# Causal mask added by VectorE instead of a matmul, maximum subtracted by GpSimd, one exponential a sequence

## Chip, cores and metric

One core of a Trainium2 chip. The metric is the device time of one execution in microseconds (us), the median of three runs. The engines are TensorE (PE in the profile, PEld for its weight loads), VectorE (DVE), ScalarE (ACT), GpSimd (POOL) and SyncE (SP), which issues the DMAs. They run their own instruction queues in order and meet through semaphores.

## What is computed

One layer on 32 sequences of 64 tokens of width 1024: a projection with a LoRA chosen by the sequence's labeler, causal attention with rotary positions (32 heads, 8 key and value heads, head width 32), an output projection with a residual, and two mixtures of LoRA experts on top of two more projections. Of it the change touches the softmax of attention:

```python
scores = jnp.einsum('bhqd,bhkd->bhqk', q, k) / math.sqrt(HEAD_DIM)
causal = jnp.tril(jnp.ones((seq_len, seq_len), dtype=bool))
scores = jnp.where(causal[None, None, :, :], scores, jnp.float32(-1e+20))
attn = jax.nn.softmax(scores, axis=-1)
out = jnp.einsum('bhqk,bhkd->bhqd', attn, v)
```

## The kernel before

The 2048 tokens are 16 units of 128 tokens, two sequences each. Four stages follow each other. First, weights that are used one after the other are multiplied into one (a fold: L368 are its matmuls). Second, attention goes unit by unit. Third, a second fold for the feed-forward part. Fourth, that part, unit by unit. A product of two float32 numbers is made of three matmuls (high by high, high by low, low by high); ACT copies the high part of a tile, and DVE or POOL subtracts it from the whole to get the low part.

The change is in stage two, `attention`. Each engine runs `step(u, main, score, value, nxt)`. In step u, unit u is projected (`main`), unit v = u-1 gets its scores and softmax (`score`), and unit w = u-2 its values (`value`). Steps 2 to 14 are a loop; steps 0, 1, 15, 16 and 17 are written out. Steps 16 and 17 project nothing more; in their place they do the first part of the second fold (`fold2.first` on PE, `fold2.low_w` on DVE, `fold2.high_w` on ACT).

PE's order in a step is fixed: for each of 8 slices k of the contraction, three parts of `project`, and ahead of some of them other work, by the table `BESIDE`: transposes of the probabilities of w (L997) at k=0 and 1, attention times values (L1012) at k=1 and 2, transposes of the rotated queries and keys of v (L968) at k=2 and 3, `scores(v,0)` (L984) at k=4 part 0, `scores(v,1)` at k=5 part 1. `project` writes banks 0 to 3 of PSUM; at k=0 its part 0 is bank 0, part 1 bank 1, part 2 banks 2 and 3. Banks 0 and 1 wait for DVE to have moved the former unit's out (`bank_out`), banks 2 and 3 for `qkv_out`. At k=7, behind part 0, PE transposes the low-rank product (`transpose_down`, L1023), for which ACT must have copied it (`down`: L738), and behind the last part `up` (L1029) adds the low-rank product into the banks. Then DVE moves the banks out with the bias (L906, three instructions; the last one signals `qkv_out`).

Scores of a sequence b are two PSUM banks (128 x 1024 values; `s_ps`). Before each bank's twelve matmuls a matmul of two constant bf16 tiles, `mask_l` and `mask_r`, writes 0 or -1e20 (L979), and the scores are added onto it. DVE then reduces the maximum (L880) and subtracts it, from PSUM into `prob` (L882, semaphore `s_sub`). `scores(v,1)` uses the same two banks, so it waits for `s_sub` of sequence 0.

ACT's part: sequence 0 is taken in 16 exponentials of 128x64 that also sum (L677, each with an accumulator read), where the step is also `main`; sequence 1 in one exponential (L679), and DVE sums it (L822). DVE inverts the sums (L824), POOL multiplies (`normalise`, L768), and PE transposes at the start of the next step. Orders around it: ACT does `exp_scores(v,0)`, `exp_scores(v,1)`, then `low` for `down` (L738), `lows` (L741), and the high parts of the next unit's input. DVE does `less_max(0)`, `less_max(1)`, both `inverse_sum`, then `lows` (L898) and the three moves of L906. POOL does the two halves of the rotation (L775, L777), `split_x`, `normalise(v,0)`, `split_a`, `split_x`, `normalise(v,1)`. DVE's work at the start of a step is `probs_low` (`pt_l`, L806) and the rotation's products (L801).

Of the kernel before, what the change touches and what calls it, by code (L numbers as in the profile page):

```python
# [502 lines left out]
def attention(nc, a, sem, keep, psum, ring, c_h, c_l, a_raw, index, fold1, fold2):  # L503
# [3 lines left out]
    def sb(name, shape, dt=F32):  # L507
# [28 lines left out]
    mask_f = prob[:, 0, :, :, :].rearrange("p g c k -> p (g c k)")  # L536
# [6 lines left out]
    const_in, index_in, mask_ready = sem("const_in"), sem("index_in"), sem("mask_ready")  # L543
# [11 lines left out]
    s_done, s_max, s_sub, s_exp, s_sum, s_inv, s_norm = (  # L555
        sem(n) for n in ("s_done", "s_max", "s_sub", "s_exp", "s_sum", "s_inv", "s_norm"))
    pt_done, pt_high, pt_low = sem("pt_done"), sem("pt_high"), sem("pt_low")
    pv_done, pv_out, stored = sem("pv_done"), sem("pv_out"), sem("attn_stored")
    consts = [(b_bc[:, :], a["b_qkv"].partition_broadcast(P)), (cos[:, :], a["cos"]), (sin[:, :], a["sin"]),
              (hmask[:, :], a["hmask"]), (ident[:, :], a["ident"]), (mask_f[:, BANK:BANK + P], a["mask_l"]),  # L560
              (mask_f[:, 0:BANK], a["mask_r"])]

    def k_tiles():
        return keys[:, :].rearrange("p (n t) -> p n t", t=SEQ)
# [91 lines left out]
    def scalar(act):  # L656
# [11 lines left out]
            act.wait_ge(pt_done, 2 * w + b + 1)  # L668
            act.activation(pt_h[:, :, :, :, :].rearrange("p q j g t -> p q (j g t)"), t_ps[:, :, :], ACT.Copy).then_inc(pt_high, 1)

        def exp_scores(v, b, sums):

            act.wait_ge(s_sub, 2 * v + b + 1)
            if sums:
                for g in range(2):
                    for c in range(KVH):
                        last = act.activation(prob[:, 0, g, c, :], prob[:, 0, g, c, :], ACT.Exp, scale=SCALE, accum_out=ssum[:, 0, g, c:c + 1])  # L677
            else:
                last = act.activation(prob[:, b, :, :, :], prob[:, b, :, :, :], ACT.Exp, scale=SCALE)  # L679
            last.then_inc(s_exp, 1)  # L680

        def step(u, main, score, value, nxt):
            v, w = u - 1, u - 2
# [42 lines left out]
            if score:  # L726
                if not main:
                    fold2.high_w(act, 5)
                    fold2.high_w(act, 6)
                exp_scores(v, 0, main)  # L730
                if not main:
                    fold2.high_w(act, 7)
                exp_scores(v, 1, False)
            if main:
                act.wait_ge(low_done, u + 1)
                for b in range(BPU):
                    rows = slice(b * SEQ, (b + 1) * SEQ)
                    last = act.activation(low4[rows, :, :], down_ps[rows, b * LR:(b + 1) * LR].unsqueeze(1).to_broadcast([SEQ, 4, LR]), ACT.Copy, scale=LORA_SCALE)  # L738
                last.then_inc(low_copied, 1)
                act.wait_ge(low_t, u + 1)  # L740
                act.activation(lows[:, :], low_ps, ACT.Copy).then_inc(low_high, 1)  # L741
            if nxt:
                high_a(act, u + 1)
                high_x(act, u + 1, 1)
# [2 lines left out]
                fold2.high_w(act, 0)  # L747

        act.wait_ge(const_in, 16 * len(consts))
        act.activation(mask_r[:, :], mask_f[:, 0:BANK], ACT.Copy)  # L750
        act.activation(mask_l[:, :], mask_f[:, BANK:BANK + P], ACT.Copy).then_inc(mask_ready, 1)
        fold2.high_chunk(act, 0, 0)
        steps(act, step)

    def gpsimd(pool):
        def split_x(u, half):
            pool.wait_ge(x_high, 2 * u + half + 1)
            pool.tensor_tensor(x_l[:, ks(half), :], x_raw[:, ks(half), :], x_h[:, ks(half), :].bitcast(F32), ALU.subtract).then_inc(x_low, 1)  # L758
# [29 lines left out]
        split_x(0, 0)  # L788
        split_a(0)
        split_x(0, 1)  # L790
        pool.wait_ge(fold1.done, fold1.TILES * fold1.chunks)
        pool.memset(vb_h[:, :, :, :, :, :].bitcast(F32), 0.0).then_inc(vb_zero, 1)
        pool.memset(vb_l[:, :, :, :, :, :].bitcast(F32), 0.0).then_inc(vb_zero, 1)
        steps(pool, step)

    def vector(dve):
# [19 lines left out]
        def row(t, b):  # L816
            return t[:, b, :, :].rearrange("p g c -> p (g c)")

        def inverse_sum(v, b, summed=False):
            dve.wait_ge(s_exp, 2 * v + b + 1)  # L820
            if not summed:
                dve.tensor_reduce(row(ssum, b), flat(b), AX.X, ALU.add).then_inc(s_sum, 1)  # L822
                dve.wait_ge(s_sum, UNITS + b if isinstance(v, int) and v == UNITS - 1 else v + 1)
            dve.reciprocal(row(sinv, b), row(ssum, b)).then_inc(s_inv, 1)  # L824

        def step(u, main, score, value, nxt):
# [28 lines left out]
            if score:  # L855
# [19 lines left out]
                    fold2.low_w(dve, 4)  # L875
                scores = s_ps[:, :, :].rearrange("p g (c k) -> p (g c) k", k=SEQ)

                def less_max(b):
                    dve.wait_ge(s_done, 2 * v + b + 1)
                    dve.tensor_reduce(row(smax, b), scores, AX.X, ALU.max).then_inc(s_max, 1)  # L880
                    dve.wait_ge(s_max, 2 * v + b + 1)
                    dve.tensor_tensor(flat(b), scores, row(smax, b).unsqueeze(2).to_broadcast([P, 2 * KVH, SEQ]), ALU.subtract).then_inc(s_sub, 1)  # L882

                less_max(0)
                if main:
                    less_max(1)
                    inverse_sum(v, 0, True)
                else:
                    fold2.low_w(dve, 5)
                    inverse_sum(v, 0)  # L890
                    fold2.low_w(dve, 6)
                    less_max(1)
            if score and main:
                inverse_sum(v, 1)
            if main:
                dve.wait_ge(low_high, u + 1)
                rows = slice(2 * LR, 3 * LR)
# [5 lines left out]
                for n in range(NCH):  # L903
                    dve.wait_ge(qkv_done, NCH * u + n + 1)
                    to, bias = (t[:, n * BANK:(n + 1) * BANK].rearrange("p (o c) -> p o c", o=2) for t in (qkv, b_bc))
                    dve.tensor_tensor(to, out[n] if n < NCH - 1 else psum[:, 2:4, 0:FCH], bias, ALU.add).then_inc(bank_out if n < NCH - 1 else qkv_out, 1)  # L906

        fold2.low_chunk(dve, 0, 0)
        steps(dve, step)

    def tensor(pe):
# [59 lines left out]
        def scores(v, b):  # L971
            if b == 0:
                pe.wait_ge(qk_low, 3 * v + 3)
                pe.wait_ge(k_low, v + 1)
                need(pe, pv_out, 2 * v)
            else:
                pe.wait_ge(s_sub, 2 * v + 1)
            for g in range(2):
                pe.matmul(s_ps[:, g, :], mask_l[:, :], mask_r[:, :], start=True, stop=False)  # L979
                for q in range(QUADS):  # L980
                    o = s_ps[:, g, q * 4 * SEQ:(q + 1) * 4 * SEQ]
                    cols = slice(q * GRP + 2 * g, q * GRP + 2 * g + 2)
                    for n, (qq, kk) in enumerate(((q_h, k_h), (q_h, k_l), (q_l, k_h))):
                        mm = pe.matmul(o, qq[:, b, cols, :].rearrange("p g t -> p (g t)"), kk[:, q, b, :, :].rearrange("p c t -> p (c t)"),  # L984
                                       start=False, stop=q == QUADS - 1 and n == 2)
            mm.then_inc(s_done, 1)

        def transpose_p(v, b):
# [626 lines left out]
```

## Time and profile before

| | |
|---|---|
| Median of 3 runs | 1226.75 us (1225.2 to 1227.36) |
| Span of the profiled execution | 1224.6 us |
| PE busy | 1199.6 us |
| DVE busy | 602.9 us |
| ACT busy | 379.0 us |
| POOL busy | 303.9 us |
| Attention steps in the trace | about 160 to 603 us, two steps of the drain until 648 us |
| One turn of the loop | 28.34 us |

The page gives busy times by engine over the whole span, and the chain of work that ended last, followed back. A timeline row is: start in us, duration in us, engine, line of the kernel, operation, what it writes from what it reads, how many instructions; in square brackets the engine's idle time just before, and whose result ended it. Rows with a count above one are merged, and PE's durations contain a latency, so that the distance between the starts of two matmuls is what one costs. A share of busy time is an average over stages, so the rows of one turn are read for this change.

### The profile page before, as it was taken

The numbers are of one execution on the slowest core, as the hardware profiler recorded it, in microseconds if no ns is written. First come the engines' busy times: TensorE is split into PE (matmuls) and PEld (weight loads), VectorE is DVE, ScalarE is ACT, GpSimd is POOL, SyncE is SP. The second block draws the span as 40 slices with busy tenths as digits, with TensorE's granted clock in tenths as the row PEclk, the third lists the DMA queues.
The fourth block names the chain that finished last, engine by engine and source line by source line (L and its number), as shares of the span: only waits on it lengthen the run. The fifth ranks groups of instructions, "written<-read, shape, count | busy, mean of one in ns | idle before, by whom it ended". The sixth has DMA issues, their size and how long they took to land.

```text
span 1224.6 us, 20268 instructions
## 1 busy us (share of the span) xinstructions
PE 1199.6 (98%) x7424; PEld 1071.1 (87%) x7440; DVE 602.9 (49%) x1173; ACT 379.0 (31%) x1157; POOL 303.9 (25%) x182
## 2 busy tenths in 40 slices
PE   7999999999999999999999999999999999999997
PEld 7999988888888888888889998888888888888886
DVE  5222136767676766777773226344443333334443
ACT  4212124455545555555543224111111111111110
POOL 0000123433433344444220002222222222222220
PEclk9999999999999999999999999999999999999999
DMA  6111032111111111110312314111111111111100
GB/s 245 35 36 51 9 121 82 44 47 56 43 48 46 43 43 43 43 52 25 119 54 87 108 70 139 53 59 59 52 51 51 51 51 51 51 51 51 51 35 34
DMA packets 30003, 74.82 MB, mean 61 GB/s; under 512 B 4114, under 2 KB 8722, under 8 KB 29970
## 3 DMA queue, kind: packets, MB, share of 16 engines
q1 hardware_dynamic: 29970, 74.36, 17.6%
q8 instruction: 23, 0.38, 0.1%
q14 instruction: 10, 0.08, 0.0%
HBM read 57.57 MB, written 16.78 MB: 61 GB/s over the span
## 4 chain that ended last, share of the span: by engine, by line
PE 93%; DVE 3%; ACT 1%; DMA 1%; issue 1%; POOL 0%; SPq 0%; DVEq 0%; ACTq 0%
PE psum L949 21%; PE psum L368 21%; PE psum L1499 19%; PE psum L1454 14%; PE psum L984 4%; PE psum L1012 4%; PE psum L1471 2%; PE psum L997 2%; PE psum L1479 2%; PE psum L968 1%; PE psum L1487 1%; PE psum L979 1%; PE psum L1029 1%; ACT low L738 1%; DVE rot_t L801 1%
## 5 line engine op out<-in xcount | busy, mean ns | idle before, releaser
L368 PE MATMUL psum<-c_high_low,w_h 128*128 128x256 f32 (+1 forms) x1344 | 238.4, 288 | 9.6 <-ACT w_h L242 8.1
L368 PEld LDWEIGHTS psum<-c_high_low,w_h 128*128 128x128 f32 x1344 | 205.0, 193 | 10.0 <-DVE c_high_low L296 8.1
L1499 PE MATMUL psum<-fr_h,c_high_low 128*128 128x512 f32 (+1 forms) x768 | 212.6, 361 | 0.1
L949 PE MATMUL psum<-p_h,c_high_low 128*128 128x512 f32 (+1 forms) x768 | 196.4, 359 | 0.5 <-DVE qkv L906 0.5
L368 PE MATMUL psum<-c_high_low,w_l 128*128 128x256 f32 (+1 forms) x704 | 177.8, 279 | 2.1 <-DVE w_l L350 2.1
L1454 PE MATMUL psum<-w_h,c_high_low 128*128 128x512 f32 x512 | 170.2, 397 | 0.8 <-DVE w_l L1279 0.8
L1499 PEld LDWEIGHTS psum<-fr_h,c_high_low 128*128 128x128 f32 x768 | 136.5, 188 | 22.6 <-issue 0.3
L949 PEld LDWEIGHTS psum<-p_h,c_high_low 128*128 128x128 f32 x768 | 134.1, 189 | 13.4 <-issue 0.7
L1499 PE MATMUL psum<-fr_l,c_high_low 128*128 128x512 f32 (+1 forms) x384 | 138.3, 360 | 0.0
L368 PEld LDWEIGHTS psum<-c_high_low,w_l 128*128 128x128 f32 x704 | 127.6, 193 | 2.3 <-DVE w_l L350 2.3
L1337 POOL TENSOR_TENSOR x_out<-x,spare 128x1024 f32<-128x1024 f32 x16 | 38.8, 2423 | 350.3 <-DMA out<-x_out 331.4
L1454 PEld LDWEIGHTS psum<-w_h,c_high_low 128*128 128x128 f32 x512 | 96.1, 188 | 23.1 <-DVE w_l L1279 1.7
L949 PE MATMUL psum<-p_l,c_high_low 128*128 128x512 f32 (+1 forms) x384 | 105.0, 368 | 0.0
L758 POOL TENSOR_TENSOR c_high_low<-ring,c_high_low 128x512 fp32r<-128x512 f32 x32 | 41.8, 1307 | 240.7 <-ACT c_high_low L643 240.7
L1454 PE MATMUL psum<-w_l,c_high_low 128*128 128x512 f32 x256 | 99.9, 390 | 0.0
L768 POOL TENSOR_TENSOR prob<-prob,sinv 128x1024 f32<-128x1024 f32 x32 | 62.7, 1960 | 140.7 <-DVE sinv L824 140.7
L1499 PEld LDWEIGHTS psum<-fr_l,c_high_low 128*128 128x128 f32 x384 | 72.2, 188 | 10.4
L949 PE MATMUL psum<-end_h,c_high_low 128*128 128x320 f32 x256 | 76.4, 311 | 0.0
L677 ACT ACTIVATE prob<-prob 128x64 f32<-128x64 f32 x240 | 57.7, 242 | 55.6 <-DVE prob L882 55.6
L949 PEld LDWEIGHTS psum<-p_l,c_high_low 128*128 128x128 f32 x384 | 67.2, 192 | 6.3
L880 DVE TENSOR_REDUCE smax<-psum 128x16 f32<-128x1024 f32 x32 | 39.2, 1224 | 58.4 <-PE psum L984 58.4
L1400 DVE TENSOR_TENSOR lb_h<-psum,lb_h 128x128 fp32r<-128x128 f32 x32 | 9.3, 292 | 117.9 <-ACT lb_h L1301 117.9
(142 smaller groups left out, 1996.5 us busy)
## 6 DMA issues: line engine op xcount, KB each, us to landing
ring<-in_x_t SPq DMA_DIRECT2D x32, 256.0 KB, 2.7
attn_scratch<-ring SPq DMA_DIRECT2D x16, 512.0 KB, 2.6
ring<-attn_scratch SPq DMA_DIRECT2D x32, 256.0 KB, 2.8
ring<-in_x_tok SPq DMA_DIRECT2D x16, 512.0 KB, 3.3
out<-x_out SPq DMA_DIRECT2D x16, 512.0 KB, 3.2
ring<-in_wqkv_t SPq DMA_DIRECT2D x12, 512.0 KB, 4.5
ring<-in_last_t SPq DMA_DIRECT2D x10, 512.0 KB, 4.8
w_raw<-in_w_cond SPq DMA_DIRECT2D x8, 512.0 KB, 9.4
```

The source lines that it names most:

```text
L368: mm = pe.matmul(to, stationary, moving, start=start and n == 0, stop=k == KT - 1 and n == len(passes) - 1, skip_group_check=True)
L677: last = act.activation(prob[:, 0, g, c, :], prob[:, 0, g, c, :], ACT.Exp, scale=SCALE, accum_out=ssum[:, 0, g, c:c + 1])
L758: pool.tensor_tensor(x_l[:, ks(half), :], x_raw[:, ks(half), :], x_h[:, ks(half), :].bitcast(F32), ALU.subtract).then_inc(x_low, 1)
L768: pool.tensor_tensor(rows, rows, sinv[:, b, :, :].rearrange("p g c -> p (g c)").unsqueeze(2).to_broadcast([P, 2 * KVH, SEQ]), ALU.mult).th ...
L880: dve.tensor_reduce(row(smax, b), scores, AX.X, ALU.max).then_inc(s_max, 1)
L949: mm = pe.matmul(to, sx[:, k, :], moving(w, n, k), start=first, stop=False, skip_group_check=True)
L984: mm = pe.matmul(o, qq[:, b, cols, :].rearrange("p g t -> p (g t)"), kk[:, q, b, :, :].rearrange("p c t -> p (c t)"), start=False, stop=q ...
L997: mm = pe.transpose(t_ps[:, q, at:at + P], prob[:, b, g, c:c + 2, :].rearrange("p c k -> p (c k)"), ident[:, :])
L1012: mm = pe.matmul(s_ps[:, b, q * 4 * SEQ:(q + 1) * 4 * SEQ], vv[:, b, q, j, :, :].rearrange("p c d -> p (c d)"), pp[:, q, j, :, :].rearrang ...
L1337: pool.tensor_tensor(x1_out[:, :], x1[:, :], bb_bc[:, :], ALU.add).then_inc(x1_biased, 1)
L1454: mm = pe.matmul(w_ps[:, n, :], s[:, k, :], w[:, k, n * BANK:(n + 1) * BANK], start=k == 0 and s is at_h and w is wo_h, stop=k == KT - 1 a ...
L1499: mm = pe.matmul(b_ps[:, n, 0:cols.stop - cols.start], s[:, k, :], w[:, k, cols], start=first, stop=n == 2 and k == KT - 1 and s is x1t_l)
```

## The change

The matmuls of the mask and their constants are gone; the first score matmul of each quad's part now starts the accumulation itself. The mask, 64 x 64, is loaded twice into `hidden`, once for the partitions of each sequence. DVE adds it while it moves the scores from PSUM to `prob` (`s_masked`), and takes the maximum from `prob`. POOL subtracts the maximum in place (`s_sub`). ACT takes one exponential for each sequence and sums nothing; DVE sums both. `scores(v,1)` on PE waits for `s_masked` of sequence 0. DVE's `inverse_sum(v,1)` moves from ahead of `lows` to between the second and the third instruction of L906. ACT's `down` and `down_high` become functions; their place in its order stays. In step 16, DVE does the add and maximum of sequence 1 ahead of `inverse_sum(v,0)` instead of last.

```diff
-    mask_l = sb("mask_l", [P, P], BF16)
-    mask_r = sb("mask_r", [P, BANK], BF16)
+    hidden = sb("hidden", [P, SEQ])
...
+    consts += [(hidden[b * SEQ:(b + 1) * SEQ, :], a["mask_r"][0:SEQ, 0:SEQ]) for b in range(BPU)]
...
-        def exp_scores(v, b, sums):
+        def exp_scores(v, b):
 
             act.wait_ge(s_sub, 2 * v + b + 1)
-            if sums:
-                for g in range(2):
-                    for c in range(KVH):
-                        last = act.activation(prob[:, 0, g, c, :], prob[:, 0, g, c, :], ACT.Exp, scale=SCALE, accum_out=ssum[:, 0, g, c:c + 1])
-            else:
-                last = act.activation(prob[:, b, :, :, :], prob[:, b, :, :, :], ACT.Exp, scale=SCALE)
-            last.then_inc(s_exp, 1)
+            act.activation(prob[:, b, :, :, :], prob[:, b, :, :, :], ACT.Exp, scale=SCALE).then_inc(s_exp, 1)
...
+        def less_max(v, b):
+            pool.wait_ge(s_max, 2 * v + b + 1)
+            rows = prob[:, b, :, :, :].rearrange("p g c k -> p (g c) k")
+            pool.tensor_tensor(rows, rows, smax[:, b, :, :].rearrange("p g c -> p (g c)").unsqueeze(2).to_broadcast([P, 2 * KVH, SEQ]),
+                               ALU.subtract).then_inc(s_sub, 1)
...
             if score:
+                less_max(v, 0)
+                less_max(v, 1)
                 normalise(v, 0)
...
-                def less_max(b):
+                def masked(b):
                     dve.wait_ge(s_done, 2 * v + b + 1)
-                    dve.tensor_reduce(row(smax, b), scores, AX.X, ALU.max).then_inc(s_max, 1)
-                    dve.wait_ge(s_max, 2 * v + b + 1)
-                    dve.tensor_tensor(flat(b), scores, row(smax, b).unsqueeze(2).to_broadcast([P, 2 * KVH, SEQ]), ALU.subtract).then_inc(s_sub, 1)
-
-                less_max(0)
+                    dve.tensor_tensor(flat(b), scores, hidden[:, :].unsqueeze(1).to_broadcast([P, 2 * KVH, SEQ]),
+                                      ALU.add).then_inc(s_masked, 1)
+                    dve.wait_ge(s_masked, 2 * v + b + 1)
+                    dve.tensor_reduce(row(smax, b), flat(b), AX.X, ALU.max).then_inc(s_max, 1)
+
+                masked(0)
                 if main:
-                    less_max(1)
-                    inverse_sum(v, 0, True)
+                    masked(1)
+                    inverse_sum(v, 0)
                 else:
                     fold2.low_w(dve, 5)
+                    masked(1)
                     inverse_sum(v, 0)
                     fold2.low_w(dve, 6)
-                    less_max(1)
-            if score and main:
-                inverse_sum(v, 1)
...
                     dve.tensor_tensor(to, out[n] if n < NCH - 1 else psum[:, 2:4, 0:FCH], bias, ALU.add).then_inc(bank_out if n < NCH - 1 else qkv_out, 1)
+                    if score and n == NCH - 2:
+                        inverse_sum(v, 1)
...
             for g in range(2):
-                pe.matmul(s_ps[:, g, :], mask_l[:, :], mask_r[:, :], start=True, stop=False)
```

## Rows read from the trace of the kernel before

**Rows 1.** The page: DVE, ACT and POOL beside PE, and the chain by engine.
```profile
PE 1199.6 (98%) x7424; PEld 1071.1 (87%) x7440; DVE 602.9 (49%) x1173; ACT 379.0 (31%) x1157; POOL 303.9 (25%) x182
...
PE 93%; DVE 3%; ACT 1%; DMA 1%; issue 1%; POOL 0%; SPq 0%; DVEq 0%; ACTq 0%
```

**Rows 2.** Busy times of one turn: stretch, length, busy (instructions) by engine, clock, DMA.
```profile
461.12:489.46 28.34, 28.23 (x180) 25.24 (x180) 19.75 (x29) 15.28 (x56) 11.40 (x8) 1.00 0.13 46
```

**Rows 3.** Timeline of PE in that turn, inside `scores(v,0)`, around one mask matmul.
```profile
477.39 0.28 PE L984 MATMUL psum<-k_h,q_l 128*128 128x256 f32 x1
477.51 0.39 PE L979 MATMUL psum<-mask_r,mask_l 128*128 128x512 bf16 x1
...
477.86 0.28 PE L984 MATMUL psum<-k_l,q_h 128*128 128x256 f32 x1
```

**Rows 4.** Timelines of the same turn: softmax of sequence 1, up to `transpose_down`.
```profile
481.17 0.26 ACT L677 ACTIVATE prob<-prob 128x64 f32<-128x64 f32 x1 [3.66 <-DVE prob L882]
...
483.46 1.22 DVE L880 TENSOR_REDUCE smax<-psum 128x16 f32<-128x1024 f32 x1 [2.32 <-PE psum L984]
...
485.86 0.24 DVE L824 RECIPROCAL sinv<-ssum 128x16 f32<-128x16 f32 x1
...
485.97 1.06 ACT L679 ACTIVATE prob<-prob 128x1024 f32<-128x1024 f32 x1 [0.87 <-DVE prob L882]
...
486.18 1.91 POOL L768 TENSOR_TENSOR prob<-prob,sinv 128x1024 f32<-128x1024 f32 x1 [7.31 <-DVE sinv L824]
...
487.07 1.22 DVE L822 TENSOR_REDUCE ssum<-prob 128x16 f32<-128x1024 f32 x1 [0.96 <-ACT prob L679]
...
487.54 0.56 ACT L738 ACTIVATE low<-psum 64x128 f32<-64x128 f32 x2 [0.51 <-PE psum L949]
488.15 0.14 PEld L1023 LDWEIGHTS psum<-ident,low 128*128 128x128 f32 x1 [0.39 <-ACT low L738]
```

**Rows 5.** Timelines of the start of a step, one engine after the other.
```profile
461.56 1.89 DVE L906 TENSOR_TENSOR qkv<-psum,b_bc 128x512 f32<-128x512 f32 x3 [0.80 <-PE psum L1029]
463.98 1.23 DVE L806 TENSOR_TENSOR pt_l<-psum,pt_h 128x1024 fp32r<-128x1024 f32 x1 [0.53 <-ACT pt_h L669]
...
463.87 0.51 PE L949 MATMUL psum<-p_h,c_high_low 128*128 128x512 f32 x2
...
463.52 1.92 POOL L768 TENSOR_TENSOR prob<-prob,sinv 128x1024 f32<-128x1024 f32 x1
```

**Rows 6.** The page's groups: line, out<-in, count, busy, mean ns, idle before.
```profile
L1337 POOL TENSOR_TENSOR x_out<-x,spare 128x1024 f32<-128x1024 f32 x16 | 38.8, 2423 | 350.3 <-DMA out<-x_out 331.4
```

**Rows 7.** Timelines of step 16, one engine after the other.
```profile
602.86 0.88 PE L1029 MATMUL psum<-pb,lows 128*128 128x512 f32 x4
...
614.79 1.22 PE L368 MATMUL psum<-c_high_low,w_l 128*128 128x256 f32 x8 [2.11 <-DVE w_l L350]
...
634.20 1.09 PE L997 MATMUL psum<-ident,prob 128*128 128x128 f32 x8 [0.42 <-POOL prob L768]
...
605.20 1.21 DVE L350 TENSOR_TENSOR w_l<-wo_raw,w_h 128x1024 fp32r<-128x1024 f32 x1
606.33 1.22 DVE L806 TENSOR_TENSOR pt_l<-psum,pt_h 128x1024 fp32r<-128x1024 f32 x1
...
626.19 1.22 DVE L880 TENSOR_REDUCE smax<-psum 128x16 f32<-128x1024 f32 x1 [0.87 <-PE psum L984]
...
631.23 1.16 DVE L350 TENSOR_TENSOR w_l<-w_raw,w_h 128x1024 fp32r<-128x1024 f32 x1
...
631.39 2.76 POOL L768 TENSOR_TENSOR prob<-prob,sinv 128x1024 f32<-128x1024 f32 x1 [17.73 <-DVE sinv L824]
```

**Rows 8.** PE's wait in step 1 (timeline), and granted clocks behind two waits (busy times).
```profile
186.67 1.74 PE L968 MATMUL psum<-ident,roped 128*128 128x128 f32 x8 [1.97 <-POOL roped L777]
...
186.67:190.66 3.99, 3.99 (x17) 3.61 (x17) 2.01 (x5) 2.85 (x7) 0.00 (x0) 0.57 0.62 247
614.79:618.07 3.28, 3.28 (x28) 3.28 (x29) 3.28 (x3) 0.59 (x2) 0.00 (x0) 1.00 0.04 9
```

More of the change, by code:

```diff
@@ L533, in attention @@
     ident = sb("ident", [P, P])
-    mask_l = sb("mask_l", [P, P], BF16)
-    mask_r = sb("mask_r", [P, BANK], BF16)
-    mask_f = prob[:, 0, :, :, :].rearrange("p g c k -> p (g c k)")
+    hidden = sb("hidden", [P, SEQ])
     out = [psum[:, n, :].rearrange("p (o c) -> p o c", o=2) for n in range(2)] + [psum[:, 2, 0:FCH], psum[:, 3, 0:FCH]]
@@ L541, in attention @@
     low_ps = t_ps[:, 1, 0:P]
-    const_in, index_in, mask_ready = sem("const_in"), sem("index_in"), sem("mask_ready")
+    const_in, index_in = sem("const_in"), sem("index_in")
     x_in = [sem("x_in0"), sem("x_in1")]
@@ L554, in attention @@
     v_high, v_low, vb_zero, vb_high, vb_low = (sem(n) for n in ("v_high", "v_low", "vb_zero", "vb_high", "vb_low"))
-    s_done, s_max, s_sub, s_exp, s_sum, s_inv, s_norm = (
-        sem(n) for n in ("s_done", "s_max", "s_sub", "s_exp", "s_sum", "s_inv", "s_norm"))
+    s_done, s_masked, s_max, s_sub, s_exp, s_sum, s_inv, s_norm = (
+        sem(n) for n in ("s_done", "s_masked", "s_max", "s_sub", "s_exp", "s_sum", "s_inv", "s_norm"))
     pt_done, pt_high, pt_low = sem("pt_done"), sem("pt_high"), sem("pt_low")
@@ L559, in attention @@
     consts = [(b_bc[:, :], a["b_qkv"].partition_broadcast(P)), (cos[:, :], a["cos"]), (sin[:, :], a["sin"]),
-              (hmask[:, :], a["hmask"]), (ident[:, :], a["ident"]), (mask_f[:, BANK:BANK + P], a["mask_l"]),
-              (mask_f[:, 0:BANK], a["mask_r"])]
+              (hmask[:, :], a["hmask"]), (ident[:, :], a["ident"])]
+    consts += [(hidden[b * SEQ:(b + 1) * SEQ, :], a["mask_r"][0:SEQ, 0:SEQ]) for b in range(BPU)]
     def k_tiles():
@@ L669, in probs_high, with down, down_high @@
             act.activation(pt_h[:, :, :, :, :].rearrange("p q j g t -> p q (j g t)"), t_ps[:, :, :], ACT.Copy).then_inc(pt_high, 1)
-        def exp_scores(v, b, sums):
+        def exp_scores(v, b):
             act.wait_ge(s_sub, 2 * v + b + 1)
-            if sums:
-                for g in range(2):
-                    for c in range(KVH):
-                        last = act.activation(prob[:, 0, g, c, :], prob[:, 0, g, c, :], ACT.Exp, scale=SCALE, accum_out=ssum[:, 0, g, c:c + 1])
-            else:
-                last = act.activation(prob[:, b, :, :, :], prob[:, b, :, :, :], ACT.Exp, scale=SCALE)
-            last.then_inc(s_exp, 1)
+            act.activation(prob[:, b, :, :, :], prob[:, b, :, :, :], ACT.Exp, scale=SCALE).then_inc(s_exp, 1)
+        def down(u):
+            act.wait_ge(low_done, u + 1)
+            for b in range(BPU):
+                rows = slice(b * SEQ, (b + 1) * SEQ)
+                last = act.activation(low4[rows, :, :], down_ps[rows, b * LR:(b + 1) * LR].unsqueeze(1).to_broadcast([SEQ, 4, LR]), ACT.Copy, scale=LORA_SCALE)
+            last.then_inc(low_copied, 1)
+        def down_high(u):
+            act.wait_ge(low_t, u + 1)
+            act.activation(lows[:, :], low_ps, ACT.Copy).then_inc(low_high, 1)
         def step(u, main, score, value, nxt):
@@ L729, in step @@
                     fold2.high_w(act, 6)
-                exp_scores(v, 0, main)
+                exp_scores(v, 0)
                 if not main:
                     fold2.high_w(act, 7)
-                exp_scores(v, 1, False)
+                exp_scores(v, 1)
             if main:
[L735 to L741, printed above, removed]
+                down(u)
+                down_high(u)
             if nxt:
@@ L749, in scalar @@
         act.wait_ge(const_in, 16 * len(consts))
-        act.activation(mask_r[:, :], mask_f[:, 0:BANK], ACT.Copy)
-        act.activation(mask_l[:, :], mask_f[:, BANK:BANK + P], ACT.Copy).then_inc(mask_ready, 1)
         fold2.high_chunk(act, 0, 0)
@@ L817, in row, with inverse_sum @@
             return t[:, b, :, :].rearrange("p g c -> p (g c)")
-        def inverse_sum(v, b, summed=False):
+        def inverse_sum(v, b):
             dve.wait_ge(s_exp, 2 * v + b + 1)
-            if not summed:
-                dve.tensor_reduce(row(ssum, b), flat(b), AX.X, ALU.add).then_inc(s_sum, 1)
-                dve.wait_ge(s_sum, UNITS + b if isinstance(v, int) and v == UNITS - 1 else v + 1)
+            dve.tensor_reduce(row(ssum, b), flat(b), AX.X, ALU.add).then_inc(s_sum, 1)
+            dve.wait_ge(s_sum, 2 * v + b + 1)
             dve.reciprocal(row(sinv, b), row(ssum, b)).then_inc(s_inv, 1)
@@ L976, in scores @@
             else:
-                pe.wait_ge(s_sub, 2 * v + 1)
+                pe.wait_ge(s_masked, 2 * v + 1)
             for g in range(2):
-                pe.matmul(s_ps[:, g, :], mask_l[:, :], mask_r[:, :], start=True, stop=False)
                 for q in range(QUADS):
@@ L984, in scores @@
                         mm = pe.matmul(o, qq[:, b, cols, :].rearrange("p g t -> p (g t)"), kk[:, q, b, :, :].rearrange("p c t -> p (c t)"),
-                                       start=False, stop=q == QUADS - 1 and n == 2)
+                                       start=n == 0, stop=n == 2)
             mm.then_inc(s_done, 1)
@@ L1004, in attend @@
                 pe.wait_ge(vb_low, v + 1)
-                pe.wait_ge(s_sub, 2 * v + 2)
+                pe.wait_ge(s_masked, 2 * v + 2)
             n = 0
@@ L1019, in transpose_down @@
                 pe.wait_ge(const_in, 16 * len(consts))
-                pe.wait_ge(mask_ready, 1)
                 pe.wait_ge(fold1.out_low, fold1.chunks * fold1.TILES)
```

## The prediction

> **What bounds the kernel now.** I read the page's busy shares and its chain first: TensorE (PE) is busy 98% of the span and carries 93% of the chain that ended last [rows 1]. Then I took one turn of the attention loop: from the first `up` matmul at 461.12 us to the next at 489.46 us it lasts 28.34 us, of which PE is busy 28.23 us at a granted clock of 1.00, with DVE at 19.75, ACT at 15.28 and POOL at 11.40 us [rows 2]. So removing PE work pays in full, and any new wait of PE costs in full. But PE runs its queue in order and meets, once in each turn, places where a result of another engine comes just in time. The timelines of the other engines around those places decide this change. I call step u the turn in which unit u is projected and unit v = u-1 gets its scores. Scores and main work meet in steps 1 to 15; step 16 has scores and the first part of the next fold.
>
> **What goes from PE.** Sixty-four mask matmuls, four in each of 16 units, one ahead of each half of a sequence's scores. Their recorded 0.39 us is latency, not a price. Between the `k_h,q_l` matmul at 477.39 and the second matmul behind it with a mask between, at 477.86, lie 0.47 us; starts of neighbours lie 0.12 us apart (477.39 to 477.51), so two gaps without the mask are 0.24, and the mask cost 0.23 us [rows 3]. Bounds: not below 0.12 (a 256-column neighbour) and not above 0.39. Per step 4 x 0.23 = 0.92 us; steps 1 to 15: -13.8 us. Step 16 keeps the 0.46 us before its first scores, the rest disappears in a wait there. The two casts of the mask on ACT and the larger mask loads were at the stage's start, where PE did not wait for them: 0.
>
> **What the softmax chain becomes.** Before, for the second sequence: scores end at e = 483.42 (DVE starts at 483.46), reduce 1.22, subtract 1.23, exponential 485.97 to 487.03 [rows 4]. After: DVE adds the mask and moves the scores (PSUM and SBUF in, SBUF out). The nearest row is the `pt_l` subtraction of the same shape, 1.23 us [rows 5]. Then the maximum from SBUF: the nearest row is `ssum`, 1.22 us [rows 4]. POOL subtracts the broadcast maximum: the nearest row is `normalise`, the same shape and the same broadcast, 1.91 us [rows 4]; only the operation differs. I take it; bounds 2.42 (POOL's pass over two full inputs of that size) [rows 6] and 1.76 (what a `normalise` took from the moment DVE let it run, 632.39 to 634.15) [rows 7]. ACT's exponential stays 1.06. The first sequence's 16 exponentials with accumulator reads end, but they ran from 481.17 to 485.10 (ACT was idle 0.87 us ahead of 485.97), off the path, so they pay nothing; nor does the earlier start of `scores(1)`, which now waits for the first DVE pass alone, 1.27 us: PE has three parts of `project` to do before it and comes later anyway.
>
> **Wait 1: `transpose_down`.** ACT holds exp(v,1) ahead of `down`, so `down` cannot start before it. Before, exp(v,1) ended at 487.03, `down` then waited for PE until 487.54, and PE's `transpose_down` came at 488.15, its weight load waiting 0.39 us [rows 4]: e + 4.73. After: e + 0.04 + 1.23 + 0.03 (add) + 1.22 (maximum) + 0.08 (DVE to POOL, as 486.10 to 486.18) + 1.91 + 0.06 + 1.06 (exp), then 0.47 until both `down` activations are out and 0.05 to PE: e + 6.15. PE's own work between e and this point doesn't change. So the wait grows by 1.42 us, in steps 1 to 15: +21.3 us. What is queued behind it is the rest of the projection and `up`; `down_high` and `lows` follow in 1.3 us as before, with ACT and DVE free.
>
> **Wait 2: the third bank of the next unit.** DVE now does `inverse_sum(v,1)` between the second and the last `qkv` move. `up` starts at U = 461.12; DVE's three moves run from 461.56 to 463.45. PE comes to the pieces of banks 2 and 3, which need `qkv_out`, in the second matmul of the pair that starts at 463.87, some 464.10, U + 2.98 [rows 5]. That leaves 0.65 us of slack. Put in between are ssum 1.22 + reciprocal 0.25, together 1.47 us. PE waits 1.47 - 0.65 + 0.05 = 0.87 us, and the restart costs 0.1 (8 matmuls after a wait took 1.22 us [rows 7]; 7 spacings of 0.12 and one latency of 0.28 [rows 3] are 1.12): 1.0 us in the starts of steps 2 to 15, 14 x 1.0 = +14.0 us. Bounds: 0.6 if the move and the reduce overlap more than the rows show, 1.2 if not at all. Behind the inserted pair on DVE stand `pt_l`, the rotation and so POOL's `rotated`; all slip by 0.9, as PE does, so they are in time as before. `normalise(v,1)` now ends at about U + 5.2, PE's `transpose_p(v,1)` comes at U + 6.1: covered by 0.9. `normalise(v,0)` is done a microsecond before the next step, behind the two subtractions: 1.8 us of slack.
>
> **POOL and DVE together.** A DVE pass with both inputs in SBUF and a POOL pass stretch one another: POOL's `normalise` at 631.39 takes 2.76 us instead of 1.91 beside DVE's `w_l` pass at 631.23, which ends at 632.39 [rows 7]. A reduce with one input isn't stretched (487.07, 1.22 us, with POOL from 486.18 to 488.09), nor a pass that reads PSUM (463.98, 1.23 us, with POOL from 463.52) [rows 4, 5]. So in the loop the new POOL passes meet only passes that let them run; in step 16 they meet `low_w`.
>
> Two places of the Trainium skill bear on this. "SBUF — State Buffer", section "SBUF: two separate sides", says that VectorE with two SBUF inputs and GpSimd exclude one another for whole instructions; by that rule, too, the loop is free of it and step 16 isn't, and the trace agrees. "GPSIMD Engine Reference", section "Engine selection", says to put elementwise passes on VectorE, GpSimd being about twice as slow; the trace says 1.91 against 1.23, 1.55 times. With an estimate by the page, 2.46 us a pass, wait 1 would be 2.0 us and the total 8 us higher, some 1262.
>
> **Step 16.** Counted from the `up` matmuls ahead of it, U = 602.86. `qkv_out` is 1.47 late. DVE's `low_w(0)`, which stood right behind at 605.20, then meets `normalise(15,1)` on POOL (U + 3.3 to 5.2) and ends at U + 6.3. The DVE chain from there to `w_l` at 614.74, for which PE waited before (614.79), slips by what its `pt_l` slips, which ended at 607.55, U + 4.69, and now ends at U + 7.4: +2.7 us. Then -0.46 for masks. From the end of `scores(0)` (DVE's reduce starts 0.04 behind it, at 626.19) to `transpose_p(15,0)` at 634.20 were 8.05 us [rows 7]. After: maximum known at 2.5; `low_w(5)` holds POOL until 3.7; subtract until 5.5; exp until 6.6. `scores(1)` ends at 4.3, its add and maximum at 6.8, then POOL subtracts for sequence 1 until 8.8 ahead of `normalise(0)`, which ends at 10.7 or, behind `low_w(6)`, at 11.7. That is +2.7 to +3.6, say 3.2. Step 16: 2.7 - 0.46 + 3.2 = +5.4 us.
>
> **Sum.** -13.8 + 21.3 + 14.0 + 5.4 = +26.9 us. The profiled execution has a span of 1224.6 us; the median of the runs is 1226.75, 2.15 above, which I leave as it is. A turn becomes 28.34 - 0.92 + 1.42 + 1.0 = 29.84 us. 1224.6 + 26.9 + 2.15 = 1253.7.
>
> **Rivals.**
> Both waits covered, faster. PE is busy 28.23 of 28.34 us, so if the chain is hidden only the masks count: -14.2, 1212.5 us. This decides at one place: `transpose_down` stays in time if less_max takes under about 0.5 us on POOL, and `qkv_out` if the inserted pair takes under 0.65. Rows at 1.91 and 1.47 speak against. 4%.
> Only one wait is real (the other is filled because an engine starts earlier than I see): without wait 2, 1239.7; without wait 1, 1232.4. In order queues speak against. 13% together.
> The clock. After PE stood 1.97 us until 186.67 the granted clock over the next 3.99 us was 0.57, so most of it at 1.2 instead of 2.4 GHz, and 0.43 x 3.99 = 1.7 us were lost [rows 8]; after a wait of 2.11 us, until 614.79, it stayed at 1.00 [rows 7, 8]. Waits of 1.4 and 0.9 us come every turn now, 4.3 us apart. If a third of the 15 turns fall to the lower level: +8.5, 1262; all: 1279. 11%, together with POOL's subtraction at its upper bound (15 x 0.51 = +7.7, 1261).
> The change does something else than it says (the mask add or the sum read at another rate): 2%, on both sides.
> My forecast, both waits: 70%, own range 1247 to 1260.
>
> **Range and chances.** The forecast's range is 1247 to 1260. With the first of the two cases of a single wait (1239.7, from 1238) and the clock or a slow POOL in part of the turns, up to 1268, no more than 2 in 10 are left out: 1238 to 1268. About 0.2% is what a measurement of this kernel can tell from no change, and no case lies within it but a mix of misses: faster 0.05, same 0.03, slower 0.92.
>
> **What would show it.** In the profile after: no L979 rows; a turn near 29.8 us; PE idle of 1.4 to 1.8 us behind ACT's `low` in each step and of 0.9 us behind DVE's `qkv`; POOL near 15.2 us in a turn with two subtractions of 1.91 us; ACT's exponentials at 1.06 us. It would be wrong if `down` started before exp(v,1) was over, if POOL's subtraction cost far less or more than `normalise`, or if the clock row fell below 1.00.

## The result, and the profile after

The changed kernel takes 1252.08 us (median of 4 runs, 1249.72 to 1252.36) against 1226.05 us of the kernel before on the same chip: 1.0205 times as long, 95% interval 1.019 to 1.0219. The forecast was 1253.7 us.

The page of the changed kernel, busy times by engine and the chain that ended last by engine:

```profile
PE 1189.5 (95%) x7376; PEld 1062.4 (85%) x7376; DVE 621.7 (50%) x1188; ACT 334.8 (27%) x690; POOL 365.8 (29%) x214
...
PE 84%; DVE 9%; POOL 3%; ACT 2%; issue 1%; DMA 1%; DVEq 0%; ACTq 0%
```

The span grew from 1224.6 to 1247.9 us, while PE's busy time fell by 10.1 us: PE now stands. Its share of the chain fell from 93% [rows 1] to 84%, and DVE, POOL and ACT took the difference. The waits by releaser over the whole span (total us, times, longest) say where PE stands, in the loop twice a turn:

```profile
PE psum L1025 <- ACT low L678: 21.5, 16, 1.4
...
PEld psum L953 <- DVE qkv L908: 14.5, 14, 1.1
...
PE psum L953 <- DVE qkv L908: 9.0, 15, 0.7
```

One turn by engine (stretch, length, busy and instructions of PE, PEld, DVE, ACT and POOL, clock, DMA), from one `transpose_down` to the next, against [rows 2]:

```profile
470.00:499.62 29.62, 27.59 (x177) 24.63 (x177) 20.79 (x30) 12.40 (x25) 15.23 (x10) 1.00 0.13 44
```

It is 1.28 us longer, with PE busy 0.64 us less. POOL's 15.23 us are the 11.40 of before and two passes of 1.91. ACT is 2.9 us lighter, which brings nothing. The clock stayed at 1.00. Now the chain behind `scores(v,1)` in this turn (timelines), to be laid beside [rows 4]:

```profile
493.33 1.22 DVE L883 TENSOR_TENSOR prob<-psum,hidden 128x1024 f32<-128x1024 f32 x1 [1.87 <-PE psum L987]
494.59 1.22 DVE L886 TENSOR_REDUCE smax<-prob 128x16 f32<-128x1024 f32 x1
...
495.89 1.91 POOL L770 TENSOR_TENSOR prob<-prob,smax 128x1024 f32<-128x1024 f32 x1 [2.45 <-DVE smax L886]
...
497.83 1.06 ACT L672 ACTIVATE prob<-prob 128x1024 f32<-128x1024 f32 x1 [3.29 <-POOL prob L770]
498.80 0.54 ACT L678 ACTIVATE low<-psum 64x128 f32<-64x128 f32 x2
...
499.39 0.33 PE L1025 MATMUL psum<-ident,low 128*128 128x128 f32 x1 [1.43 <-ACT low L678]
```

From DVE's start to PE's transpose are 6.06 us; before, 483.46 to 488.15, they were 4.69 [rows 4]. ACT's `low` has no idle time in front of it: it was queued behind the exponential, and PE stood 1.43 us for it. And the start of the next step, against [rows 5]:

```profile
501.15 1.29 DVE L908 TENSOR_TENSOR qkv<-psum,b_bc 128x512 f32<-128x512 f32 x2 [0.80 <-PE psum L1031]
502.36 1.21 DVE L825 TENSOR_REDUCE ssum<-prob 128x16 f32<-128x1024 f32 x1
503.61 0.25 DVE L827 RECIPROCAL sinv<-ssum 128x16 f32<-128x16 f32 x1
503.78 0.63 DVE L908 TENSOR_TENSOR qkv<-psum,b_bc 128x512 f32<-128x512 f32 x1
...
504.46 0.39 PE L953 MATMUL psum<-p_h,c_high_low 128*128 128x256 f32 x1 [0.59 <-DVE qkv L908]
```

DVE's three moves are torn apart by the sum and the reciprocal, and PE stands before the third bank until the last move is done, 0.59 us.

### The profile page after: what moved, and what is told of

Read it like the earlier page. It is cut to its first block, busy times and chain, and to the rows that moved or that the text cites. A ratio compares the mean times of both kernels' runs of the same rounds, so it can differ in the third digit from the quotient of the medians.

```text
span 1247.9 us, 19736 instructions
## 1 busy us (share of the span) xinstructions
PE 1189.5 (95%) x7376; PEld 1062.4 (85%) x7376; DVE 621.7 (50%) x1188; ACT 334.8 (27%) x690; POOL 365.8 (29%) x214
## 4 chain that ended last, share of the span: by engine, by line
PE 84%; DVE 9%; POOL 3%; ACT 2%; issue 1%; DMA 1%; DVEq 0%; ACTq 0%
PE psum L368 21%; PE psum L1501 18%; PE psum L953 15%; PE psum L1456 14%; PE psum L1015 4%; PE psum L987 4%; POOL prob L770 2%; PE psum L1473 2%; DVE qkv L908 2%; PE psum L1481 2%; DVE prob L883 2%; DVE smax L886 2%; PE psum L972 1%; DVE ssum L825 1%; ACT prob L672 1%
## 5 line engine op out<-in xcount | busy, mean ns | idle before, releaser
L368 PE MATMUL psum<-c_high_low,w_h 128*128 128x256 f32 (+1 forms) x1344 | 241.2, 290 | 10.8 <-DVE c_high_low L296 8.1
L368 PEld LDWEIGHTS psum<-c_high_low,w_h 128*128 128x128 f32 x1344 | 207.8, 196 | 11.2 <-DVE c_high_low L296 8.0
L953 PE MATMUL psum<-p_h,c_high_low 128*128 128x512 f32 (+1 forms) x768 | 200.2, 361 | 9.0 <-DVE qkv L908 9.0
L754 POOL TENSOR_TENSOR c_high_low<-ring,c_high_low 128x512 fp32r<-128x512 f32 x32 | 41.8, 1307 | 237.1 <-ACT c_high_low L641 237.1
L770 POOL TENSOR_TENSOR prob<-prob,smax 128x1024 f32<-128x1024 f32 x32 | 61.9, 1934 | 88.6 <-DVE smax L886 88.6
L672 ACT ACTIVATE prob<-prob 128x1024 f32<-128x1024 f32 x32 | 33.9, 1059 | 134.5 <-POOL prob L770 134.5
L1329 POOL TENSOR_TENSOR c_high_low<-ring,c_high_low 128x512 fp32r<-128x512 f32 x32 | 41.2, 1308 | 97.4 <-ACT c_high_low L1272 97.4
```

The lines of the kernel that those rows point to most:

```text
L368: mm = pe.matmul(to, stationary, moving, start=start and n == 0, stop=k == KT - 1 and n == len(passes) - 1, skip_group_check=True)
L770: pool.tensor_tensor(rows, rows, smax[:, b, :, :].rearrange("p g c -> p (g c)").unsqueeze(2).to_broadcast([P, 2 * KVH, SEQ]), ALU.subtract ...
L953: mm = pe.matmul(to, sx[:, k, :], moving(w, n, k), start=first, stop=False, skip_group_check=True)
L1329: pool.tensor_tensor(at_l[:, ks(half), :], at_raw[:, ks(half), :], at_h[:, ks(half), :].bitcast(F32), ALU.subtract).then_inc(at_low, 1)
```

## The experiments

Theory: the change takes 0.9 us of matmuls from a turn, and two places where PE's queue meets another engine's queue give it back and more; the costs come from the order in the queues and from the length of the chain, not from the amount of work. Rivals: POOL and DVE have simply too much work; or PE is slowed (clock, contention); or the mask work was hidden anyway. All medians stand beside runs of the kernel before on the same chip, 1225.81 us for the first four variants of the table and 1226.27 us for the last four. "The change's 26" is 1252.08 less 1226.05 us.

Turns are measured from `transpose_down` in step 1 to the one in step 15, divided by 14. The drain is what follows, from there to the first matmul behind the attention stage:

| kernel | step 1, step 15 (us) | turn | drain | median |
|---|---|---|---|---|
| before | 204.66, 601.53 | 28.35 | 47.1 | 1226.05 |
| changed | 203.06, 617.87 | 29.63 | 54.2 | 1252.08 |
| down_first | 201.56, 597.29 | 28.27 | 57.3 | 1232.14 |
| sum_early | 205.37, 608.77 | 28.81 | 51.7 | 1237.94 |
| no_mask (from before) | 203.88, 588.26 | 27.46 | 46.7 | 1213.34 |
| half | 204.62, 595.27 | 27.90 | 47.1 | 1219.79 |
| masks_kept | 203.87, 631.28 | 30.53 | 55.0 | 1265.59 |
| both_orders | 203.53, 607.66 | 28.87 | 54.9 | 1240.25 |
| sum_moved (from before) | 205.09, 613.41 | 29.17 | 52.6 | 1242.77 |
| subtract_on_dve | 202.49, 607.21 | 28.91 | 55.6 | 1242.50 |

### Wait 1 alone away: ACT's order

```diff
                 if not main:
                     fold2.high_w(act, 7)
-                exp_scores(v, 1)
+                    exp_scores(v, 1)
             if main:
                 down(u)
                 down_high(u)
             if nxt:
                 high_a(act, u + 1)
+            if score and main:
+                exp_scores(v, 1)
+            if nxt:
                 high_x(act, u + 1, 1)
```

> The changed kernel with ACT's order turned round in steps 1 to 15: `down`, `down_high` and `high_a` ahead of the exponential of sequence 1. Theory (two in-order waits): PE's wait of 1.43 us at `transpose_down` goes in 15 steps, -21.4 us; POOL's `split_a` now stands behind a later `normalise(v,0)` and may cost 0.2 us a turn, +3: 1234 us (1230 to 1238), PE's wait behind ACT's `low` under 0.3 us each, wait 2 (0.6 us of PE idle behind DVE's `qkv`) unchanged. Rival (POOL's two subtractions are simply too much work, wherever they stand): the chain is as long as before, 1252 us. Rival (clock or contention slows PE's own matmuls): 1252 us.

Measured: 1232.14 us (1231.65 to 1232.78), ratio 1.0053 (1.0036 to 1.007). Every engine has the same work in it as in the changed kernel, and 19.7 of the 26 us are gone (6.3 left over the kernel before). The timelines of ACT and PE in a turn:

```profile
483.62 0.56 ACT L678 ACTIVATE low<-psum 64x128 f32<-64x128 f32 x2 [2.88 <-PE psum L956]
...
485.29 1.05 ACT L672 ACTIVATE prob<-prob 128x1024 f32<-128x1024 f32 x1
...
484.23 0.33 PE L1028 MATMUL psum<-ident,low 128*128 128x128 f32 x1
...
489.30 0.39 PE L956 MATMUL psum<-p_h,c_high_low 128*128 128x256 f32 x1 [0.41 <-DVE qkv L911]
```

ACT waits for PE again, not the other way round; PE's transpose has no idle time in front. The rivals of too much work and of a slow PE gave 1252 and fall. Wait 2 is a little shorter (0.41), since PE comes later by a wait of some 0.2 us for `split_a`. The turn, 28.27 us, is even shorter than before, so the 6.3 us that are left don't come from the loop. They come from the drain, 57.3 us against 47.1: PE stands there 2.10, 2.90 and 4.52 us, and from 613.29 to 615.00 and from 638.57 to 643.00, behind the last two, its granted clock was 0.50 (timeline):

```profile
602.46 2.17 PE L368 MATMUL psum<-c_high_low,w_h 128*128 128x256 f32 x16 [2.10 <-DVE qkv L911]
...
613.29 2.08 PE L368 MATMUL psum<-c_high_low,w_l 128*128 128x256 f32 x8 [2.90 <-DVE w_l L350]
...
638.57 1.75 PE L1003 MATMUL psum<-ident,prob 128*128 128x128 f32 x7 [4.52 <-POOL prob L767]
```

### Wait 2 alone away: DVE's order

```diff
+            if score and main:
+                inverse_sum(v, 1)
             if main:
                 dve.wait_ge(low_high, u + 1)
...
-                    if score and n == NCH - 2:
-                        inverse_sum(v, 1)
```

> The changed kernel with `inverse_sum(v,1)` back ahead of `lows` on DVE, as in the kernel before. Theory: wait 2 goes, 0.75 to 0.86 us in each of 14 turns and 1.5 to 2.8 us in step 16, -12 to -15 us; the sum now runs beside `down` and makes `lows` about 0.1 us later, +1 to +2: 1239 us (1236 to 1243). Wait 1 stays at 1.43 us. Rival (all the loss is wait 1 and the rest is noise of the drain): 1252 us. Rival (the sum pushes `lows` and so `up` late by its full 1.47 us): 1252 to 1260 us.

Measured: 1237.94 us (1237.83 to 1238.37), ratio 1.01 (1.0083 to 1.0116): 13.9 us less than the change's 26. PE's wait behind `low` is as it was, there is none behind `qkv` in the loop, and `up` comes 0.08 us later (1.41 instead of 1.33 behind the transpose). Timeline of PE:

```profile
493.52 0.33 PE L1025 MATMUL psum<-ident,low 128*128 128x128 f32 x1 [1.43 <-ACT low L678]
494.93 0.96 PE L1031 MATMUL psum<-pb,lows 128*128 128x512 f32 x4
```

Turns of 29.63 (changed), 28.27 (without wait 1) and 28.81 (without wait 2) give 1.36 us for wait 1 and 0.82 us for wait 2.

### Wait 2 alone in the kernel before

```diff
-            if score and main:
-                inverse_sum(v, 1)
...
                     dve.tensor_tensor(to, ...).then_inc(bank_out if n < NCH - 1 else qkv_out, 1)
+                    if score and n == NCH - 2:
+                        inverse_sum(v, 1)
```

> The kernel before, with only `inverse_sum(v,1)` moved between the second and the third `qkv` move on DVE. Theory: wait 2 alone, 0.75 to 0.86 us in 14 turns and 1.5 to 2.8 us in step 16: +12 to +15 us, 1239.5 us (1237 to 1242). Rival (wait 2 exists only since wait 1 shifts the engines): 1226 us.

Measured: 1242.77 us (1240.55 to 1245.08), ratio 1.0128 (1.0106 to 1.0149), +16.5 us, a little above the upper end of what was expected. The turn is as expected, 0.82 us longer. The rest is in the drain, 5.5 us longer where 1.5 to 2.8 were expected: PE's 2.90 us wait for `w_l` there is followed by a stretch at the lower of its two clock levels (timeline and busy times):

```profile
629.42 2.07 PE L368 MATMUL psum<-c_high_low,w_l 128*128 128x256 f32 x8 [2.90 <-DVE w_l L350]
...
629.42:631.00 1.58, 1.58 (x7) 1.58 (x8) 1.58 (x2) 0.00 (x0) 0.00 (x0) 0.50 0.00 0
631.00:633.00 2.00, 2.00 (x11) 2.00 (x10) 1.77 (x2) 0.00 (x0) 0.00 (x0) 0.50 0.11 39
633.00:635.00 2.00, 2.00 (x11) 2.00 (x11) 0.00 (x0) 0.65 (x2) 0.00 (x0) 0.50 1.00 274
```

The profiled execution took 1244.71 us; two of the four took 1240.55 and 1240.83 us, inside what was expected, with a mean clock over the program of 0.997 and 0.999 instead of 0.995. So moving one sum of 1.47 us from a place with slack to right ahead of a move that PE waits for costs more than 1% of the kernel, without a microsecond of added work.

### The price of the mask on PE, from both kernels

From the kernel before, the masks left out (the causal mask is then missing from the scores):

```diff
-                pe.matmul(s_ps[:, g, :], mask_l[:, :], mask_r[:, :], start=True, stop=False)
...
-                                       start=False, stop=q == QUADS - 1 and n == 2)
+                                       start=n == 0, stop=n == 2)
```

> The kernel before, with the 64 mask matmuls left out and nothing else changed: the causal mask is missing from the scores. It prices what the change takes from PE. Theory (a mask matmul costs PE 0.22 us, and PE's work is paid in full): 15 x 0.89 + 0.45 = -13.8 us, 1212 us (1210 to 1215). Rival (0.39 us each, by the recorded duration): 1202 us. Rival (it hides under waits or weight loads): above 1220 us.

Measured: 1213.34 us (1212.53 to 1214.05), ratio 0.99 (0.9884 to 0.9917), -12.5 us. The turn falls from 28.35 to 27.46 us, 0.22 us for each of its four mask matmuls.

And into the changed kernel, the masks put back beside DVE's add (the reverse of that diff, with the constants of before):

> The changed kernel with the 64 mask matmuls put back on PE as well, so that the mask is added twice (the value is as good as minus infinity either way). Theory: wait 1 is counted from the end of `scores(v,1)`, so mask matmuls ahead of it lengthen the turn in full and the saving of the change is real but outweighed: +13.8 us, 1266 us (1263 to 1268). Rival (the waits have become the bound and the mask work would hide in them): 1252 to 1256 us.

Measured: 1265.59 us (1264.11 to 1267.21), ratio 1.0323 (1.0306 to 1.034), 13.3 us over the change's 26. The turn is 0.90 us longer, and PE's wait behind `low` stays at 1.42:

```profile
509.21 0.33 PE L1033 MATMUL psum<-ident,low 128*128 128x128 f32 x1 [1.42 <-ACT low L682]
```

A wait that is counted from the end of PE's own work doesn't hide that work. The saving is real in both kernels, and the rival of the hidden mask falls. The turn also adds up: 28.35 - 0.89 for the masks + 1.36 + 0.82 for the waits is 29.64 us, against 29.63 measured.

### POOL's part in wait 1

```diff
                 less_max(v, 0)
-                less_max(v, 1)
+                if not main:
+                    less_max(v, 1)
...
                 if main:
                     masked(1)
+                    dve.wait_ge(s_max, 2 * v + 2)
+                    dve.tensor_tensor(flat(1), flat(1), row(smax, 1).unsqueeze(2).to_broadcast([P, 2 * KVH, SEQ]), ALU.subtract).then_inc(s_sub1, 1)
                     inverse_sum(v, 0)
```

> The changed kernel with the subtraction of sequence 1 on DVE instead of POOL in steps 1 to 15. Theory: the chain behind `scores(v,1)` loses 0.08 + 1.91 + 0.06 and gets 0.03 + 1.22 + 0.03 us, 0.77 shorter, so wait 1 shrinks from 1.43 to 0.66 us: -11.6 us, 1240.5 us (1238 to 1243). Rival (wait 1 is all of POOL's making, and goes with it): 1231 us. Rival (POOL has nothing to do with it): 1252 us.

Measured: 1242.50 us (1238.58 to 1244.29), ratio 1.0129 (1.0103 to 1.0155), 9.8 us less than the change's 26; the turn is 0.72 us shorter. The wait halves and doesn't go:

```profile
491.61 0.33 PE L1030 MATMUL psum<-ident,low 128*128 128x128 f32 x1 [0.70 <-ACT low L680]
```

So of wait 1 one half is GpSimd in the place of VectorE (1.91 against 1.23 us for the subtraction, and the hand over to POOL). The other half is left of the pass that was added, three passes behind each other where there were two: 1.22 us, of which the 0.51 us that `low` waited for PE before [rows 4] cover a part.

### Both orders changed

The diff of ACT's order and, on DVE, `n == NCH - 1` in the place of `n == NCH - 2`.

> The changed kernel with both orders changed: on ACT `down`, `down_high`, `high_a` ahead of the exponential of sequence 1, on DVE `inverse_sum(v,1)` behind the last `qkv` move instead of ahead of it. Theory: both waits go, but the sum is then 1.5 us late for `normalise(v,1)` and delays `pt_l`; PE would wait about 0.6 us at `transpose_p(v,1)` and 0.2 us for `split_a` in each turn: turn 28.3 us, 1229 us (1224 to 1235). Rival (the costs add wherever the work stands): 1245 us or more.

Measured: 1240.25 us (1238.75 to 1240.61), ratio 1.0109 (1.0092 to 1.0126). This one I missed: 1229 was expected, up to 1235. The waits at `low` and at `qkv` are gone, and the one that was expected at the transposes of sequence 1 is not there. But the trace has new ones, in front of both groups of matmuls that read `pt_l`, 0.17 and 0.80 us (timelines of DVE, POOL, PE):

```profile
495.79 1.21 DVE L828 TENSOR_REDUCE ssum<-prob 128x16 f32<-128x1024 f32 x1
...
497.53 1.23 DVE L813 TENSOR_TENSOR pt_l<-psum,pt_h 128x1024 fp32r<-128x1024 f32 x1 [0.24 <-issue]
498.67 1.28 DVE L808 TENSOR_TENSOR roped<-qkv,cos 128x640 f32<-128x640 f32 x1
...
503.82 1.21 DVE L813 TENSOR_TENSOR pt_l<-psum,pt_h 128x1024 fp32r<-128x1024 f32 x1
...
497.37 1.90 POOL L767 TENSOR_TENSOR prob<-prob,sinv 128x1024 f32<-128x1024 f32 x1 [1.01 <-DVE sinv L830]
...
505.09 0.75 PE L1018 MATMUL psum<-pt_l,vb_h 128*128 128x256 f32 x4 [0.80 <-DVE pt_l L813]
```

I had followed the late sum through POOL, where `normalise(v,1)` is in time, and had named the delay of `pt_l` but given it no price: on DVE's own queue `pt_l(0)`, four rotation passes and `pt_l(1)` stand behind the sum. In the changed kernel they had slipped too, but PE had slipped with them, by wait 2. Now PE isn't late and waits for them instead, and the first rotation pass, which reads two SBUF tensors, runs longer into `normalise` on POOL (1.28 us; 1.04 in the changed kernel). So this order doesn't give back both waits: the length of the chain comes out at a third place. Whether another order would is not shown.

### Half of the change

Sequence 0 has 4.8 us of lead on sequence 1 (DVE starts on their scores at 502.06 and 506.85 us in the turn below). So it can take the longer chain, while sequence 1 keeps the short one.

```diff
+            with_mask = b == 1 or last_unit
...
             for g in range(2):
+                if with_mask:
+                    pe.matmul(s_ps[:, g, :], mask_l[:, :], mask_r[:, :], start=True, stop=False)
...
                 if main:
-                    masked(1)
+                    masked(0)
+                    less_max(1)
                     inverse_sum(v, 0)
+                    inverse_sum(v, 1)
```

`masked(0)` adds the mask and takes the maximum, and POOL subtracts; `less_max(1)` is maximum and subtraction on DVE, as in the kernel before.

> Sequence 0 of steps 1 to 15 by the new way (mask added by DVE, maximum subtracted by POOL, one exponential, sum by DVE), sequence 1 and all of step 16 by the old way, with its mask matmuls; `inverse_sum(v,1)` ahead of `lows`. Theory: sequence 0 has 4.8 us of lead on sequence 1, so its longer chain meets no wait of PE; half of the mask work is saved: 15 x 0.445 = -6.7 us, 1219.5 us (1217 to 1223), PE without a wait behind ACT's `low` over 0.4 us. Rival (POOL's subtraction or the added DVE sum costs wherever it stands): above 1230 us.

Measured: 1219.79 us (1218.4 to 1221.21), ratio 0.9948 (0.9931 to 0.9965): faster than both kernels, by 0.5% against the one before. One turn, and the places that matter in it (busy times; timelines):

```profile
484.96:512.87 27.91, 27.80 (x178) 25.00 (x178) 20.83 (x30) 12.40 (x25) 13.32 (x9) 1.00 0.14 47
...
510.67 1.16 DVE L836 TENSOR_REDUCE ssum<-prob 128x16 f32<-128x1024 f32 x1
511.86 0.25 DVE L838 RECIPROCAL sinv<-ssum 128x16 f32<-128x16 f32 x1
512.22 0.29 DVE L919 TENSOR_TENSOR lows<-psum,lows 32x128 fp32r<-32x128 f32 x1
...
511.55 0.33 PE L1047 MATMUL psum<-ident,low 128*128 128x128 f32 x1
```

DVE has as much work as in the changed kernel (20.83 against 20.79 us), and PE is busy 27.80 of 27.91 us. Both sums end in front of `lows`, with 0.11 us to spare. The turn is 0.45 us below that of before: two mask matmuls. The drain is that of before.

## Why the prediction was right, point by point

**The mask's price.** 0.92 us a turn forecast, 0.89 to 0.90 measured, from both kernels. Reading the distance of the starts, not the recorded 0.39 us, was what made it right.

**The passes.** Forecast from the nearest rows: add 1.23, maximum 1.22, POOL 1.91, exponential 1.06. Measured: 1.22, 1.22, 1.91, 1.06. For POOL's subtraction this case's trace sides with the row of `normalise`, not with the factor of about two of the Trainium skill ("GPSIMD Engine Reference", section "Engine selection"): beside DVE's 1.22 us of the add it is 1.57 times.

**Wait 1.** +1.42 us a turn forecast, 1.36 measured as the difference of two kernels' turns. ACT's queue was the place, and turning ACT's order round removes it.

**Wait 2.** 1.0 us forecast, 0.82 measured, from both kernels. This term was too big by 0.18 us, 2.5 us over 14 turns, and it is the one that was mis-sized in the loop. The inserted pair overlaps its neighbours on DVE: the last move ends 3.68 us behind `up` (504.41 to 500.73) where it ended 2.33 behind it before, so it delays `qkv_out` by 1.35, not by 1.47 us. PE goes on 0.05 us behind that, as forecast, and the first matmul with values comes 4.63 us behind `up` instead of 3.78 (505.36 and 464.90). Of these 0.85 us a few hundredths come back at `pt_l`, for which the weight loads wait 0.19 instead of 0.25 us a turn. The idle time of 0.9 us that was named as a sign is 0.59 in the row above: PE is 0.75 us late there, and the recorded end of the matmul ahead contains the latency.

**Step 16 and what follows.** +5.4 us forecast. Measured from the last `transpose_down` to the first matmul after the attention stage: 617.87 to 672.11 against 601.53 to 648.59, +7.2 us. Its parts (timelines of PE, DVE and POOL, and busy times with the clock):

```profile
623.03 3.63 PE L368 MATMUL psum<-c_high_low,w_h 128*128 128x256 f32 x16 [2.09 <-DVE qkv L908]
...
633.87 1.22 PE L368 MATMUL psum<-c_high_low,w_l 128*128 128x256 f32 x8 [2.05 <-DVE w_l L350]
...
656.50 1.46 PE L1000 MATMUL psum<-ident,prob 128*128 128x128 f32 x8 [4.51 <-POOL prob L764]
...
652.97 1.73 DVE L350 TENSOR_TENSOR w_l<-w_raw,w_h 128x1024 fp32r<-128x1024 f32 x1
...
653.57 2.88 POOL L764 TENSOR_TENSOR prob<-prob,sinv 128x1024 f32<-128x1024 f32 x1
...
658.00:660.00 2.00, 2.00 (x11) 2.00 (x11) 0.95 (x1) 1.02 (x1) 0.00 (x0) 0.50 0.00 0
```

Up to the end of the wait for `w_l` +2.74 us (2.7 forecast). PE's clock fell in that part too: 16 matmuls from 623.03 took 3.63 us, 2.18 before. That cost nothing, because DVE sets when `w_l` is there: in the kernel with only the sum moved the clock stayed up at this place, PE waited 2.90 us instead of 2.05, and the matmul behind the wait came 16.01 us behind the last `transpose_down`, 16.00 here. From there to the transposes +3.22 us against the 2.74 of the forecast (3.2 less the masks): `low_w(6)` got ahead of `normalise(15,0)`, the upper end that was named, and PE stood 4.51 us. The missing 1.2 us come behind that: PE's clock stood at the lower of its levels for some 3 us after the long wait, and 16 matmuls from 657.61 took 3.43 us, 2.15 before. The rival of the clock was weighed for the loop, where nothing of it came (1.00 in the turn); it was not put into step 16, and that is the term that failed there.

**Sum.** -0.44 us at the first `transpose_down` (it stands between 176.1 and 177.2 us in all ten kernels), -1.2 us from there to the second (+0.5 forecast), +17.9 in 14 turns (21 forecast), +7.2 in the drain (5.4 forecast), -0.2 in the rest: +23.3 us of span, 3.6 less than forecast. The -1.2 was in no term of the forecast: before, the clock fell behind the 1.97 us wait of step 1 [rows 8]; in this execution of the changed kernel PE stood 1.97 us at the same place and the clock stayed at 1.00. The medians differ by 26.0 us, mostly because the profiled execution is the fastest of the four, 2.4 us below their median; its mean clock is 0.997, that of the others 0.995 to 0.996. So the +26.9 us fit the medians partly by luck: a wait 2 sized too large made up for a drain sized too small, and the forecast put the median 2.15 us above the span, where it lay 4.2 above.

**The rivals.** Both waits covered (1212.5): leaving out the masks alone gives 1213.3 us, so that rival was priced rightly, but both waits are there. One wait only: 1239.7 and 1232.4 were forecast, and the kernels that ran without wait 2 and without wait 1 took 1237.9 and 1232.1 us. The second agreement is partly chance: the turn without wait 1 is 0.15 us shorter than the forecast's terms give (28.34 - 0.92 + 1.0), and its drain is 10 us longer than before, where 5.4 were forecast.

## What to carry to other kernels

Where one engine is busy nearly all of the time (98% here), price a change by the places where its queue meets another's: take the slack there from the timeline, and ask of each pass that the change adds or moves which entry of the busy engine stands behind it in that queue. Here the longer chain was free where there was lead (4.8 us, sequence 0), and where there was little (0.5 us, sequence 1) all beyond that was paid; the change paid only when it was made where the lead is. Undoing both orders without shortening the chain moved the wait to the next meeting point. And look at the stages ahead of and behind the loop by themselves: in one variant the whole loss stood in the drain.

## What the runs showed of the hardware that I had not expected

The clock: in the loop of the changed kernel PE stood 1.43 and about 0.6 us in every turn of 29.6 us, and the granted clock stayed at 1.00 in all 14 of them. Behind a wait of 4.51 us it fell to 0.50 (the row above), behind one of 2.90 us too, in two kernels, for over 5 us in one of them; behind waits of 2.0 to 2.1 us it fell in some places (623.03) and not in others (633.87), and behind the 1.97 us of step 1 it fell before the change and not after it. What makes the difference between these stays open.

A multiplication and a subtraction with a broadcast operand cost GpSimd the same 1.91 us for 128x1024 values, against 2.42 us for two full operands [rows 6].
